# A decoder's second cross attention: row maxima of two heads by one VectorE instruction

## What is computed

```python
q = (x @ Wq + bq).reshape(1, B * N, H, hd)          # 2048 tokens, 16 heads of 16
kv = (cond @ Wkv + bkv).reshape(1, -1, 2, H, hd)    # 512 context tokens
...
q, k, v = _fq_sym(q, axis=-1), _fq_sym(k, axis=-1), _fq_sym(v, axis=2)
attn = jnp.einsum('bhqd,bhkd->bhqk', q, k)
attn = jax.nn.softmax(attn.astype(jnp.float32), axis=-1)
attn = _fq_unsigned(attn, axis=-1)                  # round(attn / (max / 255)) * (max / 255)
out = jnp.einsum('bhqk,bhkd->bhqd', attn, v)
out = jnp.transpose(out, (0, 2, 1, 3)).reshape(B, N, C)
return out @ Wp + bp
```

## Time and profile before

| | us |
|---|---|
| median of 3 runs | 1352.47 (1352.17 to 1355.17) |
| the profiled execution | 1349.05 |
| its span on the core | 1347.3 |
| DVE busy in the span | 920.2 (68%) |
| TensorE busy | 1132.5 (84%) |
| ACT busy | 635.7 (47%) |
| POOL busy | 580.3 (43%) |

### The profile page before, as it was taken

One profiled execution on the slowest core, in us unless ns is written; L12 is line 12 of the kernel. 1 busy time (PEld: TensorE's weight loads), 2 busy tenths in 40 slices (PEclk: granted clock), 3 DMA queues, 4 the chain that ended last, 5 costly groups with the idle time before them and its releaser, 6 DMA issues.

```text
span 1347.3 us, 26429 instructions
## 1 busy us (share of the span) xinstructions
PE 1132.5 (84%) x8459; PEld 872.8 (65%) x8459; DVE 920.2 (68%) x2501; ACT 635.7 (47%) x1433; POOL 580.3 (43%) x885
## 2 busy tenths in 40 slices
PE   3699988994999999668887677877778788899998
PEld 2577766773999999556665444555555554688855
DVE  5576773776344444488877399999999974666657
ACT  3165654331312211325454399988889861433310
POOL 6143542246322222215555354466655654355510
PEclk8799999996999999779889789988989878999999
DMA  5775743213211111265441300000000004455555
GB/s 138 197 212 144 208 120 129 71 50 107 58 48 48 48 48 49 83 184 154 111 119 39 115 16 1 2 34 33 26 21 24 31 33 145 112 165 160 156 184 152
DMA packets 75813, 127.22 MB, mean 94 GB/s; under 512 B 11703, under 2 KB 59063, under 8 KB 72279
## 3 DMA queue, kind: packets, MB, share of 16 engines
q1 hardware_dynamic: 62142, 95.13, 25.7%
q0 software_dynamic: 10272, 28.39, 5.8%
q10 hardware_dynamic: 3264, 2.01, 0.5%
HBM read 76.97 MB, written 48.13 MB: 93 GB/s over the span
## 4 chain that ended last, share of the span: by engine, by line
PE 55%; issue 12%; POOL 10%; ACT 9%; DVE 6%; DMA 5%; SPq 1%; ACTq 1%; POOLq 0%; DVEq 0%
PE ps L228 17%; PE ps L1208 11%; PE ps L1195 7%; ACT work L1947 6%; PE ps L1179 5%; POOL work L1981 4%; PE ps L482 3%; POOL xs_scratch L1543 2%; PE ps L1164 2%; DMA W<-work 2%; PE ps L464 1%; PE ps L495 1%; PE ps L300 1%; DMA W<-q_parts 1%; DVE work L608 1%
## 5 line engine op out<-in xcount | busy, mean ns | idle before, releaser
L1559 POOL DMA_INDIRECT ys_scratch<-work x118 | 120.6, 1022 | 244.1 <-DVE work L1468 115.1
L1947 ACT ACTIVATE work<-ps,work 128x512 f32<-128x512 f32 x256 | 205.8, 826 | 39.9 <-POOL work L1981 38.9
L1885 DVE TENSOR_REDUCE work<-ps 128x1 f32<-128x512 f32 x256 | 172.8, 681 | 13.0 <-PE ps L1792 12.2
L608 DVE TENSOR_REDUCE work<-ps 128x2 f32<-128x512 f32 (+1 forms) x192 | 127.5, 685 | 73.6 <-PE ps L464 71.9
L790 POOL TENSOR_SCALAR_AFFINE_SELECT work<-work 128x256 f32<-128x256 f32 (+1 forms) x192 | 92.6, 485 | 160.5 <-ACT work L721 159.0
L1981 POOL TENSOR_SCALAR work<-work 128x1 f32<-128x1 f32 x256 | 100.0, 390 | 125.7 <-DVE work L1885 111.4
L1208 PE MATMUL ps<-work,SM 128*128 128x128 f32 x1248 | 147.7, 277 | 0.3 <-issue 0.3
L1208 PEld LDWEIGHTS ps<-work,SM 128*128 128x128 f32 x1248 | 144.4, 194 | 0.7 <-issue 0.7
L721 ACT ACTIVATE work<-ps 128x512 f32<-128x512 f32 x192 | 110.6, 598 | 67.8 <-PE ps L482 67.3
L1792 PE MATMUL ps<-SM,work 128*128 128x512 bf16 x256 | 106.2, 417 | 37.8 <-ACT work L1947 33.1
L1195 PE MATMUL ps<-W,work 128*128 x470 | 121.0, 380 | 0.0
(11 more groups left out here) (265 smaller groups left out, 2528.1 us busy)
## 6 DMA issues: line engine op xcount, KB each, us to landing
work<-xs_scratch SPq DMA_DIRECT2D x79, 132.0 KB, 2.2
W<-ys_scratch SPq DMA_DIRECT2D x16, 512.0 KB, 3.9
q_parts<-work SPq DMA_DIRECT2D x48, 128.0 KB, 1.9
W<-in_w_in SPq DMA_DIRECT2D x6, 1024.0 KB, 11.6
W<-q_parts SPq DMA_DIRECT2D x15, 384.0 KB
work<-xs_scratch SPq DMA_DIRECT2D x39, 130.0 KB, 2.1
W<-k_parts SPq DMA_DIRECT2D x8, 512.0 KB
W<-in_w_out SPq DMA_DIRECT2D x1, 4096.0 KB, 18.9
```

Of the source, the lines that this page charges most:

```text
L608: q.e.tensor_reduce(self.m[:, j, h0:h0 + n], ov, AX, ALU.max).then_inc(*up("mx", L, b, u))
L1559: q.e.indirect_dma_start(YS[L], bass.IndirectOffsetOnAxis(ap=self.dst[n % self.NY], axis=0), self.YB[n % self.NY], None).then_inc(*landing ...
L1885: q.e.tensor_reduce(self.mm[:, h:h + 1], PS[banks.of["c1_s", t, h]][:, :], AX, ALU.max, negate=True).then_inc(*up("c1_mx", t, h))
L1947: q.e.activation(self.ee[n // 2 % 3][:, 512 * (h % 2):512 * (h % 2) + 512], PS[banks.of["c1_s", t, h]][:, :], ACT.Exp, bias=self.nb[:, h:h ...
```

## The change

The eight PSUM tensors of one bank become four of two banks, and `PS` becomes views of them, one for each bank as before. In the second cross attention one VectorE instruction reads two neighbouring banks, as 128 x 2 x 512, and writes two maxima; it waits for the second score of the pair. It stands in even rounds, for units i - 2 and i - 1. The signal of the maxima counts pairs, and both biases of a pair wait for the same value. The four banks of scores in turn are now the pairs (2, 3) and (4, 5), tensors `ps1` and `ps2`.

```diff
--- before.py
+++ after.py
@@ -151,7 +151,8 @@
         def sb(name, shape, dt=F32):
             return ctx.enter_context(nc.sbuf_tensor(name, shape, dt))
 
-        PS = [ctx.enter_context(nc.psum_tensor(f"ps{i}", [128, 512], F32)) for i in range(8)]
+        P2 = [ctx.enter_context(nc.psum_tensor(f"ps{i}", [128, 1024], F32)) for i in range(4)]
+        PS = [P2[i // 2][:, 512 * (i % 2):512 * (i % 2) + 512] for i in range(8)]
         PB = [p[:, :].bitcast(BF) for p in PS]
 
         x = sb("x", [128, T, D])
@@ -1881,8 +1882,10 @@
                 e.tensor_scalar(qf, qf, MAGIC, MAGIC, ALU.add, ALU.subtract).then_inc(*up("c1_qr", t))
 
             def dve_max(self, q, t, h):
-                q.wait_ge(at("c1_s", t, h), at("c1_nb", t - 1, h), *ends(4))
-                q.e.tensor_reduce(self.mm[:, h:h + 1], PS[banks.of["c1_s", t, h]][:, :], AX, ALU.max, negate=True).then_inc(*up("c1_mx", t, h))
+
+                bk = banks.of["c1_s", t, h]
+                q.wait_ge(at("c1_s", t, h + 1), at("c1_nb", t - 1, h + 1), *ends(4))
+                q.e.tensor_reduce(self.mm[:, h:h + 2], halves(P2[bk // 2][:, :]), AX, ALU.max, negate=True).then_inc(*up("c1_mx", t, h // 2))
 
             def dve_round(self, q, n):
 
@@ -1907,8 +1910,8 @@
                 queries, rank = [self.dve_queries(q, 0)], []
                 steps(queries, 99)
                 for i, (t, h) in enumerate(self.rounds):
-                    if 1 <= i < self.N + 1:
-                        self.dve_max(q, *self.unit(i - 1))
+                    if 2 <= i < self.N + 2 and i % 2 == 0:
+                        self.dve_max(q, *self.unit(i - 2))
                     if 5 <= i < self.N + 5 and i % 2:
                         self.dve_round(q, i // 2 - 2)
                     if h == 7 and 2 <= t < T + 2:
@@ -1977,7 +1980,7 @@
                                   ALU.min, ALU.max).then_inc(*up("c1_Q3", t))
 
             def pool_nb(self, q, t, h):
-                q.wait_ge(at("c1_mx", t, h), at("c1_sq", t), at("c1_exp", t - 1, h))
+                q.wait_ge(at("c1_mx", t, h // 2), at("c1_sq", t), at("c1_exp", t - 1, h))
                 q.e.tensor_scalar(self.nb[:, h:h + 1], self.mm[:, h:h + 1], self.sq[t % 2][:, h:h + 1], LN255, ALU.mult, ALU.add).then_inc(
                     *up("c1_nb", t, h))
```

## The result

The changed kernel takes 1384.19 us (median of 4 runs, 1377.61 to 1385.23), the kernel before 1353.82 us in the same comparison. The ratio on record is 1.0194, with a 95% interval of 1.017 to 1.0218, which is 23 to 29.5 us; the two medians lie 30.4 us apart (1.022), just above it. The forecast was slower by 8.8.

A forecast was written before the change was run, and what follows sets the result against it. It took VectorE to bound the second cross attention. Even tiles' loss of 1.5 or 1.0 us less 0.2 gained gave 1.1 per two tiles, times eight 8.8 us; with 3.4 to the median, 1361.3 us, range 1346 to 1370.

The forecast's parts named there:

- The prediction's walk: Second cross attention, tile 6, heads 8 to 15: delayed biases and lock-outs cost the even tile 1.5 us, mildly 1.0.
- The clipping: On POOL, clipping of the next queries, queued behind bias 9, starts 1.2 us late and delays transposes and score 13.
- Those eight pairs come out even: Odd tile on DVE: six pairs gain about 0.4 us, one breaks even, the last gives 0.4 us back.
- The saving: DVE queue: a merged maximum occupies 1.14 us against 1.20 for two, saving 0.06 us a pair, 7.7 us in all.
- The lock-outs: DVE's rounding and POOL's work exclude each other; a locked-out bias takes about 0.6 us where it otherwise takes 0.26.
- the main signs: DVE busy down 15 to 20 us, idle before roundings above 10, ACT's bias wait above 38.9, odd tiles' stretch not longer.
- The shorter queue: First rival: in the stage the full DVE decides, so the merge makes it faster, 1344.8 us or down to 1333; chance 0.22.
- gain and delay: Second rival: the even tile loses only the 1.0 us that two tiles' 16 pairs save; 1352.5 us, chance 0.15.
- The third rival: Closed chain maxima, bias, exponential, rounding delays every light pair, five more per even tile losing 0.17 us: 1368 us, chance 0.13.

The follow-up runs named there:

- the run with both other edits: Kernel before with single maxima moved to the changed kernel's place and both biases waiting for the second maximum, maxima not merged: 1378.4 us, ratio 1.0182.
- The run that should have priced them: Changed kernel with both biases of a pair computed on DVE right behind the maxima, not on POOL: 1389.0 us.
- the five-bank pair: Kernel before with five score banks, one taken from the shared pair: 1456.34 us; the same with both biases waiting for the second maximum: 1462.13 us.

## Why the prediction was right and wrong

**The direction and the even tile.** The prediction's walk through heads 8 to 15 of an even tile gave 1.5 us. The even tile shown above lost 2.2, the eight of them 1.6 in the mean. Counted from the start of the pair (8, 9), it put the pair (12, 13) at 5.7 us, the rounding of (12, 13) at 9.6 and that of (14, 15) at 11.7; the trace after has 6.25, 10.3 and 12.35 (917.14 to 923.39, 927.45 and 929.49). The places of the waits were right (score 13, exponential 13), and each came 0.5 to 0.7 us later than the walk had it. The clipping came where the walk put it: 2.36 us behind the start of the pair (8, 9), 919.50 to 917.14. Of the 0.5 us that score 13 was later than that, most arose on TensorE, whose clock was low for longer. But the clipping is a small part of the cause: taking it out of the way gave back 4.5 us of the stage, 3.4 of them in this stretch of the even tiles, which lost 12.6 there.

**The step that failed: "Those eight pairs come out even".** This is the prediction's account of the odd tile. It took the odd tile's queue as full, so that a shorter one would only gain, and looked for an awaited exponential only at its last pair. The gain is there, up to round 13: 12.46 us for 12.70, the 0.06 us a pair that was forecast. But the maxima of the even heads now stood behind that full queue, and the biases of the pair (8, 9) came late from it. On POOL the statistics' power, the clipping and the indirect DMA's issue stand behind bias 9 and ahead of bias 10. So exponential 10 came 2.2 us late, and the pairs behind round 13, which have little on DVE, waited: 0.45 us for a score, 0.44 for POOL, 1.00 and 0.66 for exponentials. The walk was made through the even tile only; it should have been made through the odd tile too, on POOL as well as on DVE. Two tiles in the middle lost 4.15 us where 1.1 were forecast. Over the stage the stretch behind round 13 lost 12.6 us in even tiles, where eight times 1.5 is 12, and 14.8 in odd ones, where nothing was forecast: that is most of the way from 8.8 to 29.1.

**The saving.** The merged maximum lasts 1.216 us (1.23 forecast) and occupies the queue 1.13 us, from 928.22 to 929.35 in the timeline after (1.14 forecast). What it is worth is not 7.7 us but 1.8 or nothing, by the run with both other edits: the queue is no longer what bounds the stage.

**The lock-outs.** They decide much of the walk, but most of them were there before: all biases together take 100.0 us before and 108.5 after. The run that should have priced them shows only what they and POOL's queue are worth together. Of the main signs that the prediction named most came true: the roundings' idle time grew from 3.9 to 25.8 us, the maxima's busy time fell by 17.1, ACT's wait for biases rose to 61.9; that the odd tiles' stretch would not grow is the one that failed.

**The rivals.** The shorter queue decided nothing, and gain and delay did not cancel. The Trainium skill's "Perfetto Trace Analysis" (section "Optimizing Scalar/DVE Operations") says that larger operations can help a saturated engine, and that breaking instructions up can help where an engine that is not saturated leaves others waiting. Here the engine was saturated (19.65 of 20 us) and the larger operation did not help: the stage went from 321.6 to 350.7 us, and the engine was full only as long as the others were fed in time. The third rival, the closed chain over two pairs, comes nearest: its time was 1368, but it had the loss in the remaining pairs of even tiles, where there was next to none (0.18 us in four pairs). What the runs leave open is how much of the late bias's 19.2 us is the ring of four banks and how much the order of the queues: both fit the run with three banks, and the five-bank pair has too poor a base.

## What to carry to other kernels

Where an engine is full and the others wait for its results in turn, price the latency of each result before the instructions saved: here a bias later by one head's maximum cost 19 us of the stage, a maximum behind one more step 16, and one instruction for two saved 1.8 or nothing. When an instruction is moved, look at what it is moved behind in the busiest stretch and not only in the quiet one, and at what stands behind its result in the queues of the other engines. And compare parts of the span by a row that begins and ends them, since the rest of this program scatters by 12 us.

## What the runs showed that was not expected

The kernel before tolerates little in this stage: a rounding one pair later costs it 35 us (1390.57 us), a bank less 35 us (1388.24 to 1352.99 us), a bank moved from the shared pair to the scores 100 us. The same later rounding gives the changed kernel 11.3 us of its stage back. So an edit that helps one of the two kernels may well harm the other.
